# Far key blocks scored with the relative table's last row added to the keys: a sandwich of attention and a low-rank feed-forward on one core

## The reference

```
x = x + layernorm(attention(layernorm(x)))
x = x + layernorm(ffn(layernorm(x)))

attention:  q, k, v = linear(x) in 16 heads of 16
            idx = r[None, :] - r[:, None] + 511          # key position - query position + 511
            rel = rel_emb[idx]                           # the table has 1023 rows
            qk  = q.k / 4 + einsum('bhld,lrd->bhlr', q, rel)
            out = linear(softmax(qk) . v)
ffn:        base linear + shared low-rank + 2 of 6 routed low-rank experts, gated
```

## Time and profile before

| what | value |
|---|---|
| median of 3 runs | 5952.92 us (5951.9 to 5957.06) |
| the profiled execution, its own time | 5973.55 us |
| its span, first to last instruction | 5971.8 us |
| mean granted TensorE clock | 0.994 of full speed |
| PE busy | 5815.1 us, 97% |
| PE weight loads busy | 5385.6 us, 90% |
| DVE busy | 4903.6 us, 82% |
| ACT busy | 3069.3 us, 51% |
| POOL busy | 3328.2 us, 56% |

### The profile page before, as it was taken

The page is one execution under the profiler, slowest core; times in us unless marked ns, Lnnn a source line. Parts: engine busy times, 40 slices in busy tenths (PEclk is TensorE's granted clock), DMA queues, the critical chain, the costliest instruction groups (busy, mean ns, idle before and its releaser), DMA issues.

```text
span 5971.8 us, 378300 instructions
## 1 busy us (share of the span) xinstructions
PE 5815.1 (97%) x161792; PEld 5385.6 (90%) x161792; DVE 4903.6 (82%) x10178; ACT 3069.3 (51%) x5160; POOL 3328.2 (56%) x5182
## 2 busy tenths in 40 slices
PE   6999999999999999999999999999999999999997
PEld 5999999999999999999999899999999999999996
DVE  5888888888888888888888888888888888888886
ACT  3555555555555555555555555555555555555554
POOL 4555555555555555555555555555555555555555
PEclk8999999999999999999999999999999999999998
DMA  5343343443434334343343434334344343433432
GB/s 152 85 102 94 91 116 85 106 102 86 113 91 115 88 87 114 93 110 90 92 110 90 112 94 100 95 90 117 83 107 100 89 110 90 116 87 88 113 95 53
DMA packets 1461087, 589.65 MB, mean 99 GB/s; under 512 B 1127168, under 2 KB 1425136, under 8 KB 1459376
## 3 DMA queue, kind: packets, MB, share of 16 engines
q1 hardware_dynamic: 1454752, 562.48, 37.8%
q10 hardware_dynamic: 4624, 2.60, 0.2%
HBM read 476.43 MB, written 89.85 MB: 95 GB/s over the span
## 4 chain that ended last, share of the span: by engine, by line
PE 83%; DVE 10%; issue 3%; DVEq 2%; POOL 1%; SPq 0%; POOLq 0%; DMA 0%; ACT 0%
PE sc L730 21%; PE pw L757 15%; PE sc L747 15%; PE sc L724 14%; DVE r L1185 5%; PE pm L778 4%; PE pw L778 4%; PE pm L738 4%; PE pw L764 3%; DVE xn L1099 2%; DVE nmm L1197 1%; DVEq L1196 1%; DVE y2n L1099 1%; PE pm L797 1%; DVEq L1095 1%
## 5 line engine op out<-in xcount | busy, mean ns | idle before, releaser
L1185 DVE TRANSPOSE_TENSOR_REDUCE r<-sc 128x32 f16<-128x1024 f32 x2048 | 2542.9, 1242 | 22.3 <-PE sc L730 19.0
L1018 ACT ACTIVATE prob<-sc 128x1024 f32<-128x1024 f32 x2048 | 2098.8, 1025 | 213.9 <-PE sc L747 176.9
L730 PE MATMUL sc<-rm,tw 128*128 128x48 f16 (+1 forms) x49152 | 2144.6, 194 | 11.6 <-issue 11.4
L730 PEld LDWEIGHTS sc<-rm,tw 128*128 128x128 f16 x49152 | 1754.4, 100 | 13.6 <-issue 13.2
L724 PE MATMUL sc<-qm,ks 96*128 96x64 f16 x32768 | 1635.8, 193 | 23.2 <-POOL rm L592 13.8
L747 PE MATMUL sc<-nmm,pick 128*128 128x64 f16 x32768 | 1297.5, 193 | 40.5 <-DVE nmm L1197 32.1
L724 PEld LDWEIGHTS sc<-qm,ks 96*128 96x128 f16 x32768 | 1298.3, 98 | 35.2 <-issue 21.9
L1194 DVE TENSOR_REDUCE nm<-pm 16x32 f16<-16x256 f32 x2048 | 834.8, 408 | 557.5 <-PE pm L738 540.9
L747 PEld LDWEIGHTS sc<-nmm,pick 128*128 128x128 f16 x32768 | 1128.7, 98 | 179.2 <-DVE nmm L1197 91.3
L757 PE MATMUL pw<-prob,vs 128*32 128x128 f32 x32768 | 1117.9, 276 | 12.5 <-issue 8.1
L757 PEld LDWEIGHTS pw<-prob,vs 128*32 128x32 f32 x32768 | 840.1, 109 | 76.0 <-issue 14.6
(11 more groups left out here) (153 smaller groups left out, 5766.2 us busy)
## 6 DMA issues: line engine op xcount, KB each, us to landing
raw<-qk_s SPq DMA_DIRECT2D x3096, 64.0 KB, 2.9
tw<-tw_s SPq DMA_DIRECT2D x512, 288.0 KB, 4.0
v_s<-vpad SPq DMA_DIRECT2D x136, 256.0 KB, 3.4
vs<-v_s SPq DMA_DIRECT2D x64, 512.0 KB, 4.4
qm<-qk_s SPq DMA_DIRECT2D x768, 32.0 KB, 2.1
ks<-qk_s SPq DMA_DIRECT2D x378, 64.0 KB, 3.4
qk_s<-qkh SPq DMA_DIRECT2D x272, 64.0 KB, 2.9
qk_s<-qkl SPq DMA_DIRECT2D x272, 64.0 KB, 2.6
```

The lines of the kernel that those rows point to most:

```text
L730: last = mm(out3[:, :, OCT * m + q:OCT * m + q + n], tw[:, s, jp, u:u + P], rm[:, i, m, r * H:(r + n) * H].rearrange("p (h e) -> p h e", e=n),
L1018: A(prob[:, jp % 2, :, :, i * IW:(i + 1) * IW], sc[:, 2 * buf:2 * buf + 2, :].rearrange("p c (h i) -> p c h i", i=IW), ACT.Exp).then_inc(s ...
L1185: v.tensor_reduce(r1[:, 0:2 * H], sc[:, 2 * buf:2 * buf + 2, :].rearrange("p c (h i) -> p (c h) i", i=IW), axis=AX.X, op=ALU.max, apply_tr ...
```

## The change

The key blocks that lie at least 5 blocks behind the query block (`FAR`) are scored with keys that have the table's last row added. These keys are made once per batch and tile (GpSimd, `far_keys`), stored to a scratch of their own (`kf_s`), and loaded once per batch (`load_far`) into `kf`; TensorE then leaves the 12 relative products of such a block out. The body of the loop becomes 24 tiles, run 5 times, and the six tiles that remain are written out behind it.

```diff
-UNROLL = 14 * NBUF
+UNROLL = TPB * NBUF
+TURNS = (NT - 2) // UNROLL
+FAR = MAX_LEN // P + 1
+NF = TPB - FAR
...
+        kf = sb("kf", [ROWS, H // 2, NF * P], f16)
+        rfar = sb("rfar", [P, 1])
+        kfb = sb("kfb", [P, 2, P])
+        kfh = sb("kfh", [P, 2, P], f16)
+        kfl = sb("kfl", [P, 2, P], f16)
...
-            with nc.Fori(2, NT, UNROLL, engines=(eng.engine,), hint_back_edge=True) as t:
+            with nc.Fori(2, 2 + TURNS * UNROLL, UNROLL, engines=(eng.engine,), hint_back_edge=True) as t:
                 for k in range(UNROLL):
                     tile(t + k, t + (k + TPB), att=True, proj=True, a=True, b=True, ph=2 + k)
+            for t in range(2 + TURNS * UNROLL, NT):
+                tile(t, t + TPB, att=True, proj=True, a=True, b=True, ph=t)
...
+            def store_far(b, it):
+
+                for part, src in ((0, kfh), (1, kfl)):
+                    dst = kf_s[part, b].rearrange("(c p) t -> p c t", p=P)
+                    sp.dma_start(dst[:, :, (it - FAR) * P:(it - FAR + 1) * P], src[:, :, :]).then_inc(s_kfst, 16)
+
+            def load_far(b):
+                for s in range(2):
+                    for k, part in enumerate(SPLIT_ST):
+                        r = (3 * s + k) * HD
+                        src = kf_s[part, b].rearrange("(h s d) t -> s d h t", s=2, d=HD)
+                        sp.dma_start(kf[r:r + HD, :, :], src[s, :, :, :]).then_inc(s_kf, 16)
...
                             load_keys(b, NJP - 1)
+                            after(s_kfst, b * (32 * NF) + 32 * NF)
+                            load_far(b)
...
+                    if it >= FAR:
+                        after(s_kfs, b * NF + (NF + it - FAR + 1))
+                        store_far(b + 1, it)
...
+                if k >= FAR:
+                    sp.wait_ge(s_kfs, k - FAR + 1)
+                    store_far(0, k)
...
+                if jp == 1:
+                    sp.wait_ge(s_kfst, 32 * NF)
+                    load_far(0)
...
+            def far_keys(stored):
+
+                if stored is not None:
+                    pool.wait_ge(s_kfst, stored)
+                g.tensor_tensor(flat(kfb[:, :, :]), flat(qkb[:, 2:4, :]), rfar[:, :].to_broadcast((P, 2 * P)), ALU.add)
+                pool.drain()
+                split([flat(kfh[:, :, :]), flat(kfl[:, :, :])], flat(kfb[:, :, :]), s_kfs)
...
                     split([flat(qkh[:, :, :]), flat(qkl[:, :, :])], flat(qkb[:, :, :]), s_qks)
+                    if ph % TPB >= FAR:
+                        far_keys(batch_of(t) * (32 * NF) + 32 * (NF + ph % TPB - FAR))
...
+                if k >= FAR:
+                    if k == FAR:
+                        pool.wait_ge(s_rfar, 16 * TPB)
+                    far_keys(32 * (k - FAR) if k > FAR else None)
                 split([flat(first_h[k % 2][:, :, :]), flat(first_l[k % 2][:, :, :])], flat(qkb[:, :, :]), s_qksp)
...
+                it, qb = ph % TPB, ph % 2
+                far = 2 * jp + c - it >= FAR
...
+                    keys = kf[:, h, j - FAR * P:j - FAR * P + P] if far else ks[:, h, j:j + P]
+                    last = mm(bank[:, 2 * h * IW:(2 * h + 2) * IW], keys,
                               qm[:, qb, 2 * h:2 * h + 2, i * IW:(i + 1) * IW],
                               start=(h == 0), stop=False, skip_group_check=True)
+                if far:
+                    return last
...
+                        if ph % TPB == 0 and g == FAR // 2 * NI:
+                            pe.wait_ge(s_kf, batch_of(t) * 96 + 96)
...
+            for k in range(TPB):
+                act.dma_start(rfar[k * HD:(k + 1) * HD, :], relT[:, NREL - 1:NREL],
+                              allow_slow_non_contiguous=True).then_inc(s_rfar, 16)
```

More of the change, by code:

```diff
@@ L53, in sandwich_kernel @@
     qk_s = nc.dram_tensor("qk_s", (2, 2, B + 1, D, L), f16, kind="Internal").ap()
+    kf_s = nc.dram_tensor("kf_s", (2, B + 1, D, NF * P), f16, kind="Internal").ap()
     v_s = nc.dram_tensor("v_s", ((B + 1) * TPB, P, H * 32), f32, kind="Internal").ap()
@@ L208, in sandwich_kernel @@
         s_vs = [sem(f"s_vs{j}") for j in range(NJP)]
+        s_rfar = sem("s_rfar")
+        s_kfs = sem("s_kfs")
+        s_kfst = sem("s_kfst")
+        s_kf = sem("s_kf")
         s_raw = sem("s_raw")
@@ L305, in batch_of @@
             return t // TPB
-        assert (NT - 2) % UNROLL == 0
         def passes(eng, tile):
@@ L529, in _ @@
             sp.wait_ge(s_qkst, (NT + TPB) * 64)
+            sp.wait_ge(s_kfst, (B + 1) * 32 * NF)
             sp.wait_ge(s_vst, (NT + TPB) * 16)
@@ L715, in _, with scores @@
             mm = nc.tensor.matmul
-            def scores(g, c, buf, qb):
+            def scores(g, c, buf, ph):
                 jp, i = divmod(g, NI)
+                it, qb = ph % TPB, ph % 2
+                far = 2 * jp + c - it >= FAR
                 bank = sc[:, 2 * buf + c, :]
@@ L723, in scores @@
                 for h in range(H // 2):
-                    last = mm(bank[:, 2 * h * IW:(2 * h + 2) * IW], ks[:, h, j:j + P],
+                    keys = kf[:, h, j - FAR * P:j - FAR * P + P] if far else ks[:, h, j:j + P]
+                    last = mm(bank[:, 2 * h * IW:(2 * h + 2) * IW], keys,
                               qm[:, qb, 2 * h:2 * h + 2, i * IW:(i + 1) * IW],
                               start=(h == 0), stop=False, skip_group_check=True)
+                if far:
+                    return last
                 for m in range(IW // OCT):
@@ L887, in tile @@
                             pe.wait_ge(s_exp, free)
-                        scores(g, 0, buffer(ph, g), ph % 2)
+                        scores(g, 0, buffer(ph, g), ph)
                     if read is not None:
@@ L893, in tile @@
                     if att:
-                        scores(g, 1, buffer(ph, g), ph % 2).then_inc(s_scores, 1)
+                        scores(g, 1, buffer(ph, g), ph).then_inc(s_scores, 1)
                     wide(t, n, g, att, proj, a)
```

## The result

The changed kernel takes 5923.12 us (median of 4 runs, 5920.45 to 5928.48) beside 5954.99 us for the kernel before on the same chip (4 runs, 5951.9 to 5958.65): a ratio of 0.9947, with a 95% interval from 0.9930 to 0.9965, so 32 us less. The forecast was 23 us less.

A forecast was written before the change was run, and what follows sets the result against it. PE is busy almost throughout, but VectorE was taken to bound what shorter PE work returns: -55 + 14 + 5 + 9 + 4 = -23 us, from a median of 5952.9 to 5930 us, range 5885 to 5970.

The forecast's parts named there:

- VectorE, not all PE time: Far tiles: only VectorE's idle in the last groups is usable, -55 us; rival that all PE time returns, -106, chance 0.06.
- what the second block of a group gives: Last pair, g12 to g15: each block's 0.36 us counts until VectorE's idle is used; tile 1 1.23, tile 2 0.90 us.
- Tile 0: Query tile 0: gains as tile 1 plus 0.36 us in g10 from block 5, 1.59; 1.3 after late loads.
- The 0.43 us of issue in g14: A gap in g14 put down to issue; if it closed too, tile 1 would gain 1.66 us instead of 1.23.
- nothing in g14 and g15: Last two groups of a tile: VectorE runs without idle and PE waits for it, so shorter PE work gains nothing.
- GpSimd's far keys: Tiles 5 to 7: three added operations, 2.0 us, hold VectorE some 0.3 us per tile, +14 us; bounds 0 and 64.
- The rival that holds VectorE twice: g6 of tiles 5 to 7: copy and mask product each catch a whole GpSimd operation, 64 us instead of 14; chance 0.18.
- The queue and the loads: Tile 0: load bursts +5 us, xr 0.3 us late per batch; rival of 26 and tile 0's gain lost, chance 0.22.
- what would make me wrong: Signs: tile 1 at 42.4 us, tiles 5 to 7 at 46 or more, PE waiting for far keys, GpSimd for xr.
- Before the loop: First batch: far keys made one at a time delay the second pair's keys by 9.4 us, +9; between 2 and 12.
- The 24-tile body: Loop: 5 turns instead of 3, two more jumps back at about 2 us each, +4 us; between 3 and 6.
- The lower bound of the gain: Far tiles: -35 us if the two small idle times are not to be had and tile 0 gives 1.0.

The follow-up runs named there:

- e2: Changed kernel with all far-key work (made, stored, loaded) but no product left out, all blocks scored the old way: 5970.9 us, 1.0016 against the kernel before.
- e3: Changed kernel with relative products left out only for far blocks in a pair's first bank (block 6): 5940.14 us, 0.9965 against the kernel before.
- e4: Changed kernel with relative products left out only for far blocks in the second bank (5 and 7): 5948.87 us, 0.9982 against the kernel before.
- e7: Changed kernel with the second feed-forward layer's product in g12 written to bank pw instead of the maxima's bank: 5903.22 us, 0.9911 against the kernel before.
- e8: Changed kernel with one more 128x128 GpSimd operation in the far keys of tiles 5 to 7: 5950.42 us, 0.9983 against the kernel before.
- e6: Changed kernel with the last pair's keys loaded at the end of tile 1 instead of in tile 0: 5913.46 us, 0.9927 against the kernel before.
- e9: Changed kernel with far keys reordered before the loop, last pair's keys loaded in tile 1, and g12's feed-forward product in pw: 5874.35 us, 0.9855 against before.
- e1: Kernel before with only the 24-tile loop body (5 turns, six tiles written out), no far keys: 5959.95 us, 1.0003 against the kernel before.

## Why the prediction was right, and where it was wrong

The direction and the size were right (-32 for -23), the size in part by luck. Of the terms, the gain was put 14 us too high and the costs 22 too high.

**VectorE, not all PE time: right in its main line.** 4608 products of 30 ns would be 138 us, and they gave 41 (e2 to after). VectorE's timeline in a tile 1 after, g11 to g15, answers to the earlier trace rows:

```profile
2698.81 0.41 DVE L1257 TENSOR_REDUCE nm<-pm 16x32 f16<-16x256 f32 x1 [1.17 <-PE pm L796]
...
2701.36 0.41 DVE L1257 TENSOR_REDUCE nm<-pm 16x32 f16<-16x256 f32 x1 [0.69 <-PE pm L796]
...
2703.86 0.41 DVE L1257 TENSOR_REDUCE nm<-pm 16x32 f16<-16x256 f32 x1
...
2706.64 0.41 DVE L1257 TENSOR_REDUCE nm<-pm 16x32 f16<-16x256 f32 x1
...
2708.98 0.85 DVE L1162 TENSOR_SCALAR y2n<-y,mv,rs 128x256 f32<-128x256 f32 x1
...
2711.53 0.89 DVE L1162 TENSOR_SCALAR xn<-x,mv,rs 128x256 f32<-128x256 f32 x1
```

The idle times of g12 and g13 (0.41 and 0.18) are gone, as forecast. That of g11 shrank from 1.02 to 0.69, where I had written 0.38.

**The step that failed: what the second block of a group gives.** I took 1.23 us for tile 1 and 0.90 for tile 2, and announced tiles of 44.0 and 44.4 us; their medians are 44.97 and 45.34. By group medians, tile 1 gives 0.34 in g11, 0.34 in g12, 0.13 in g13, and loses 0.09 in g14: 0.72. Tile 2 gives 0.11 in g13 and loses 0.08 in g14: nothing. I had read only the engine that I took for the bound: where VectorE is idle for the transposes, every cut in PE's work was to shorten that idle time. But the transposes stand between the banks in PE's order. Products left out behind them first bring PE earlier to its next wait. In g12 that is L836, which waits for the reduction of the very maxima that came too late, and in g13 L815, which waits for the exponential. PE in the same tile 1:

```profile
2701.83 0.83 PE L836 MATMUL pm<-w_base,x1T 128*128 128x256 f16 x6 [0.27 <-DVE nm L1257]
...
2704.57 1.08 PE L815 MATMUL pw<-prob,vs 128*32 128x128 f32 x32 [0.51 <-ACT prob L1081]
...
2710.49 0.64 PE L805 MATMUL sc<-nmm,pick 128*128 128x64 f16 x16 [0.94 <-DVE nmm L1260]
```

e3 and e4 show it from both sides: the even bank alone leaves tile 1 with g11, g12 and g13 just as after has them (2.55, 2.50, 2.78), the odd one alone with the old values in g11 and g12 (2.89, 2.84), and 2.79 in g13. e7 takes the first of the two waits away, and g12 of tile 1 goes from 2.50 to 2.31, of tile 2 from 2.84 to 2.40. That the second wait would give back the rest was not tried.

**Tile 0: 1.59 forecast without the late loads, 1.61 measured by group medians, for the wrong reasons.** Its last pair gives less, as in tile 1. Block 5, for which I had counted 0.36 in g10 alone, gives 0.22 in g9, 0.37 in g10 and 0.31 more in g11. I had written that g9 is without idle; there is some, and block 5, also an odd one, lies in a stretch where I see no side product of PE that waits for VectorE (that this is the reason is argued, not shown). Two errors of the same size cancelled. The mean, with the late loads in it, fell by 1.50 for 1.3.

**The 0.43 us of issue in g14 is in no tile 1.** I had read it in tile 19 and allowed that it closes in tiles 1 and 0. It stands in tiles 19, 61 and 103 of the kernel before, once in each turn of the loop, and the trace after has it in tile 19 too, and in four more, 24 tiles apart. In a tile 1 of before (tile 17) g14 looks so:

```profile
898.57 0.77 DVE L1099 TENSOR_SCALAR y2n<-y,mv,rs 128x256 f32<-128x256 f32 x1
```

There is no gap ahead of it, and y2n takes 0.77 us, not the 0.41 of tile 19; this is so in 14 of the 15 tiles 1 behind the first batch. After, it takes 0.85 in 10 of them, which is the 0.09 that g14 loses, and 0.51 to 0.53 in the other five, whose g14 takes 2.77 to 2.80. GpSimd masks the next windows at that time (2707.97 to 2709.68 in the tile 1 shown). In e7 VectorE's rows are these:

```profile
2702.72 0.38 DVE L1165 TENSOR_SCALAR y2n<-y,mv,rs 128x256 f32<-128x256 f32 x1
...
2704.80 0.38 DVE L1165 TENSOR_SCALAR xn<-x,mv,rs 128x256 f32<-128x256 f32 x1
```

Both are down to 0.38, though GpSimd masks then too; y2n now starts 0.86 us behind the first mask (2701.86) instead of 1.01. The median g14 and g15 are 2.64 and 2.64 instead of 3.11 and 2.96. So "nothing in g14 and g15" was not VectorE's own bound, but in part a matter of which of the two engines came first.

Taken instruction by instruction, the traces give the rule for y2n beside masks. It never ends sooner than some 0.15 us behind the end of the mask operation in which it starts. Where it starts 0.06 us into one of 0.67, it takes 0.75 to 0.77; 0.21 to 0.25 into one of 0.61, it takes 0.55 to 0.51; 0.40 into it, 0.38, the time that it has without GpSimd. Where it starts 0.54 to 0.56 into it, so within 0.08 of its end, it is held until 0.15 us behind the end of the next, and takes 0.83 to 0.86. The y2n of before, after and e7 fit this, and so do their xn, the other operation of this shape. In 10 of the 15 tiles 1 of e7, y2n starts 0.40 us into such an operation, where it costs nothing; in the other five it starts 0.21 into one and takes 0.55.

This is also why e7 gave twice what was expected. By means over the tiles, after to e7: g12 and g13 of tiles 0 and 1 give 9 us and tile 2 gives 7; g14 and g15 of tiles 0 and 1 give 9, which I had not counted; and g12 of all other tiles goes from 2.89 to 2.80, 0.09 in each of 80, 7 us more, so that product had cost something in every tile. That makes 32, where the two traces differ by 25 and the timed runs by 21. g4 of tile 0 is 3 us longer in all, and tiles 3 to 7 gain 4 us and not 7; what made these is not known. New waits for the exponential, in g15 of tiles 1, which takes 3.7 to 4.7 us in four of them, are in the 32 already.

**GpSimd's far keys: +14 forecast, nothing measured.** GpSimd and VectorE in a tile 7 after:

```profile
2957.19 0.61 POOL L652 TENSOR_TENSOR kfb<-qkb,rfar 128x256 f32<-128x256 f32 x1
2957.95 0.61 POOL L644 TENSOR_TENSOR kfh<-kfb,one 128x256 f16<-128x256 f32 x1
2958.70 0.67 POOL L646 TENSOR_TENSOR kfl<-kfb,kfh 128x256 f16<-128x256 f32 x1
```

```profile
2958.53 0.17 DVE L1296 COPY best<-order 128x2 f32<-128x2 f32 x1
...
2959.41 0.18 DVE L1260 TENSOR_TENSOR nmm<-nm,mask_h 16x64 f16<-16x64 f16 x1
```

The copy starts 0.03 us before GpSimd's second operation ends (2957.95 + 0.61) and is over before the third begins; the mask product starts behind it. Neither is held. The forecast had placed the copy in the second operation too, some 0.3 us further from its end; the first one takes 0.61, not the 0.67 that I had used. With e8's half microsecond more the same copy does meet one:

```profile
2969.50 0.61 POOL L644 TENSOR_TENSOR kfh<-kfb,one 128x256 f16<-128x256 f32 x1
```

```profile
2969.54 0.60 DVE L1299 COPY best<-order 128x2 f32<-128x2 f32 x1
```

It takes 0.60 instead of 0.17 and costs the kernel 21 us. The rival that holds VectorE twice was real as a mechanism and lost by position. The Trainium skill (page SBUF — State Buffer, section SBUF: two separate sides) says that GpSimd and a VectorE instruction that is in a two-port mode or has two SBUF inputs exclude each other, and that the later one stands still until the other's instruction is over. The copy's 0.60 us agrees with that, and so do the times of y2n above, all tied to the end of a GpSimd operation; only the rows tell whether the two meet.

**The queue and the loads: 5 for bursts and 5 for late loads forecast; 7 us in tile 0 of e2, and 3 more in tile 1.** I had counted 8 of the 16 tiles 7 of before with a gap of over 1.2 us; by PE's idle time it is six. And I had looked for the new bursts in tile 0 alone. The loads cost the next tile too: by means, g0 and g2 of tile 1 take 2.59 and 2.98 us after, 2.36 and 2.68 before. That is 0.5 us in a tile whose last groups gain 0.72 by their medians. The two have different causes. The excess of g2 is 1.0 to 1.6 us in three tiles 1. In one of them PE stands between two blocks:

```profile
3399.67 0.39 PE L780 MATMUL sc<-qm,ks 96*128 96x64 f16 x8 [1.44 <-issue]
```

In e7, where the loads lie as after, the two groups take 2.58 and 2.88. In e6, which moves the keys, they are back at 2.36 and 2.70, in e9 at 2.42 and 2.67. The excess of g0 stands in four tiles 1, each behind a stop in g15 of tile 0, and the clock has a part in it (below). GpSimd waits five times for xr, 7.3 us in all and 1.9 at most, and PE three times for a window, 1.8 us in all. An example, on GpSimd, then on PE:

```profile
3024.70 0.72 POOL L728 TENSOR_TENSOR x<-yn,xr 128x256 f32<-128x256 f32 x1 [1.80 <-DMA xr<-x]
```

```profile
3027.27 0.64 PE L805 MATMUL sc<-nmm,pick 128*128 128x64 f16 x16 [2.14 <-DVE nmm L1260]
3028.45 0.55 PE L780 MATMUL sc<-qm,ks 96*128 96x64 f16 x8 [0.55 <-DMA tw<-tw_s]
```

So of what would make me wrong, "GpSimd waits for xr" did occur, in 5 of 16 batches, at the size that the sum had for it. PE never waited for far keys.

**The clock: forecast to stay at its upper level (2.4 GHz), and it didn't quite.** In the kernel before it is granted at that level from 95 to 5925 us without a break. After, it falls to the lower one (1.2 GHz) for 3.4 to 6.8 us behind four of the five stops in g15 of tile 0 (1.7 to 2.3 us long; the fifth has 1.4), and at one jump and the exit of the loop. The view by windows of the first, behind a stop of 2.27 us that ended at 858.17 (stretch, us, busy time of PE, PEld, DVE, ACT, POOL, granted clock, DMA share, GB/s):

```profile
858.00:865.00 7.00, 6.32 (x107) 6.11 (x108) 3.88 (x6) 2.65 (x4) 6.86 (x14) 0.54 0.79 217
```

The g0 that follow take 2.86 to 3.75 us instead of 2.37, 3.7 in all; how much of it is the clock and how much the late inputs is not taken apart. In e6, without these stops, the clock stays up in tiles 0 and 1. So a late load costs more than the wait for it.

**Before the loop: +9 forecast, +13.7 measured.** The two parts that were worked out held: g4 of the first tile at 95.55 for 96.5, with GpSimd waiting until the far stores had landed:

```profile
60.67 0.61 POOL L652 TENSOR_TENSOR kfb<-qkb,rfar 128x256 f32<-128x256 f32 x1 [6.39 <-DMA kf_s<-kfl]
```

The rest is mostly the stop of 3.9 us at 111.45, where I had put no burst: from 105 to 113 us the view by windows gives the DMA engines a share of 1.26, and 0.82 of the full clock. But the 13.7 are one trace against one. In the other traces with the same loads before the loop the first tile ends between 132.3 and 137.4 us, so the term is 9 to 14, and its excess over the forecast is not sure. In e2 the same stretch costs 13.1 us of its trace, while all its costs over several runs are 9.5 (4 to 15 by its interval); I can't say which of the other terms is smaller than its trace shows.

**The 24-tile body: +4 forecast, +2 measured** with 5 us of interval on either side (e1). Single places show what a turn's end can cost: the tile at the loop's exit takes 49.99 us, 4.7 more than an undisturbed one. In the table this stands partly against the -3.6 behind the last maximum.

**The sum.** Gain 41 instead of 55, costs 9.5 instead of 32: -32 instead of -23. The forecast came this near because the two errors have opposite signs, and that is luck. The lower bound of the gain, put at -35, adds up to -32 by its own terms.

## What to carry to other kernels

Where one engine's work between two waits gets shorter, look at its next wait in its own order, not only at the idle time of the engine that you take for the bound: a side product that shares a bank with the critical transposes swallowed the second block's 0.36 us, and giving it another bank was worth 21 us. What GpSimd's operations cost VectorE here was a matter of position: 2 us of them per tile cost nothing, and the same shifted by half a microsecond cost 20 us over 48 tiles. A gap read in one tile needs a look at its like before it goes into a sum: the 0.43 us came once in a turn of the loop. Moving six old loads out of the burst with the new ones took away every wait for a late input in tile 0, and made 12 us, which alone is not clear of noise.

## What the runs showed of the hardware that I had not expected

- A VectorE copy of two elements per partition took 0.17 us beside GpSimd's work when it began 0.03 us before the end of a GpSimd operation that another followed only 0.14 us later, and 0.60 when it began 0.04 us behind the start of one.
- A VectorE operation of 128x256 took 0.38 to 0.89 us while GpSimd masked windows, by where it started: it ended no sooner than some 0.15 us behind the end of the mask operation that ran, or of the next one when it started in about the last 0.08 us. The reductions from PE's accumulators (0.41) and the transposed maxima (1.23 to 1.25) kept their times beside the same operations.
- PE stood for 1.5 to 4.2 us within one block of sixteen matmuls that wait for nothing, in nine traces with the far keys, where the view by windows gives the DMA engines a share of 0.9 to 1.3 over 8 us; the two kernels without far keys had no such stop there (0.48 from 100 to 113 us in before). Six loads fewer did not settle it: 1.71 us in e6 and 2.82 in e9, beside 1.53 in e3 with all of them. The page has queues of instructions among those of the DMA engines (20.55 MB in after), so instructions that come late are a candidate; this was not tried.
- The granted clock fell to its lower level for 3.4 to 6.8 us behind single stops of PE of 1.7 to 2.3 us, in a kernel that keeps PE busy for 96% of its span. Behind stops of up to 2.1 us in tiles 7 of the kernel before it did not.
